# A graph and expert kernel: the second node stage joined with the making of its slot table, counts kept per tile

## What is computed

```
x = x + relu(segment_sum(norm * (layernorm(x) @ W.T + b)[row], col))
n = layernorm(x)
logits = einsum('td,hde->hte', n, hash_proj)      # 4 hashes, 64 experts
cand = argmax(logits, -1)                         # one candidate for a hash
sel = the candidates of the 2 best scores of the 4
pos = cumsum(one_hot(sel), axis=0) - 1            # place in its expert, tokens in order
keep = pos < C
y = gelu(n @ W1[e]) @ W2[e]                       # e = sel, kept ones only
x = x + mean over the 2 of y
```

## Time and profile before

| | us |
|---|---|
| median of 3 runs | 2936.8 (2929.69 to 2940.85) |
| the profiled execution, its time | 2943.63 |
| its span | 2941.9 |
| first node of the second node stage gathered (POOL) | 1726.38 |
| last entry of slot_tokens ends | 2266.93 |
| first gather of the expert stage | 2293.18 |

### The profile page before, as it was taken

How to read it: one execution, slowest core, us unless ns; L and a number is a source line. 1 busy time by engine, 2 the same in 40 slices (tenths; PEclk the granted TensorE clock), 3 DMA queues, 4 the chain that set the end, 5 groups by cost and what they waited for, 6 DMA issues and landing times. The chain is left out here.

```text
span 2941.9 us, 43922 instructions
## 1 busy us (share of the span) xinstructions
PE 2220.5 (75%) x11763; PEld 1308.8 (44%) x11789; DVE 1821.7 (62%) x5128; ACT 920.2 (31%) x2016; POOL 1789.1 (61%) x2143
## 2 busy tenths in 40 slices
PE   8999999857777728999978859999992677773000
PEld 3444444335555516666644436666661344442000
DVE  4776766524444459999921126777774477666666
ACT  1111111024445415777753315555552000000000
POOL 4555555566666348888536624777775555553776
PEclk9999999969898959999989979999996699897555
DMA  6655555468888646788669956666751799995999
GB/s 204 223 189 180 190 185 181 145 191 249 255 258 267 206 142 198 255 264 262 206 210 353 361 185 204 213 215 215 215 176 44 224 366 363 341 307 196 346 374 340
DMA packets 361398, 698.60 MB, mean 237 GB/s; under 512 B 51609, under 2 KB 85235, under 8 KB 361153
## 3 DMA queue, kind: packets, MB, share of 16 engines
q1 hardware_dynamic: 239672, 399.69, 40.0%
q0 software_dynamic: 76720, 217.93, 23.8%
q10 hardware_dynamic: 44761, 78.17, 7.5%
HBM read 426.08 MB, written 287.17 MB: 242 GB/s over the span
## 5 line engine op out<-in xcount | busy, mean ns | idle before, releaser
L2085 POOL DMA_INDIRECT xg<-n_rows,ids x219 | 218.3, 997 | 158.7 <-PE psum L154 81.1
L148 PE MATMUL psum<-wl,xT 128*128 128x512 f32 x632 | 288.8, 599 | 0.0
L148 PE MATMUL psum<-wg,yT 128*128 128x512 f32 x632 | 286.7, 597 | 0.0
L148 PE MATMUL psum<-wr,xT 128*128 128x512 f32 x632 | 284.1, 592 | 0.0
L2235 POOL DMA_INDIRECT q<-slot_outputs,qs x158 | 173.4, 1097 | 86.7 <-issue 47.9
L337 ACT ACTIVATE xb<-xa,xsc 128x512 f32<-128x512 f32 x79 | 64.2, 814 | 480.7 <-POOL xsc L397 480.6
L1637 POOL DMA_INDIRECT slot_tokens<-sl x158 | 169.1, 1070 | 66.0 <-issue 60.4
L154 PE MATMUL psum<-ident,xg 128*128 128x128 f32 x876 | 152.3, 308 | 71.6 <-issue 34.1
L384 POOL TENSOR_TENSOR ve<-mv,epst 128x1 f32<-128x1 f32 x79 | 51.0, 645 | 254.1 <-DVE mv L439 254.1
L2173 DVE COPY gT<-psum 128x512 f32<-128x512 f32 x219 | 142.0, 685 | 101.3 <-PE psum L154 54.2
L684 POOL DMA_INDIRECT gl<-xl_rows,idx x118 | 129.9, 1101 | 112.5 <-DVE vv L736 65.1
(11 more groups left out here) (320 smaller groups left out, 5497.2 us busy)
## 6 DMA issues: line engine op xcount, KB each, us to landing
slot_outputs<-yo ACTq DMA_DIRECT2D x54, 1024.0 KB
x_rows<-x SPq DMA_DIRECT2D x158, 256.0 KB
edge_sums<-eo SPq DMA_DIRECT2D x29, 1056.0 KB
edge_sums<-go SPq DMA_DIRECT2D x29, 1024.0 KB
xT<-in_xTt SPq DMA_DIRECT2D x79, 256.0 KB
xl_rows<-xl SPq DMA_DIRECT2D x79, 256.0 KB
xr_rows<-xr SPq DMA_DIRECT2D x79, 256.0 KB
residual_rows<-xb SPq DMA_DIRECT2D x79, 256.0 KB
```

Of the source, the lines that this page charges most:

```text
L148: last = nc.tensor.matmul(ps, lhs[:, k, :], rhs[:, k, :], start=(k == 0), stop=(k == DK - 1))
L2085: pool.indirect_dma_start(xg[:, t % 8, :], None, XN3, bass.IndirectOffsetOnAxis(ids[:, t:t + 1], 0), bounds_check=NP - 1, oob_is_err=False ...
```

## The change

- The slot table is made inside the second node stage: VectorE's 29 operations behind its last tile, reading the total of counts straight from TensorE's result (the copy cnt goes); POOL's two gathers of idr behind its last entry; TensorE's turning behind its last tile. One `end_phase` stands behind all.
- idr and xg are cleared at the beginning of the node stage, ahead of POOL's first gather of edge sums; the expert stage has no clearing.
- The sum of a group's rows (`counted`) goes. `count_up` keeps a running count for each tile, four small additions a group, cum having four places. So `before` has two products for a group, 256 columns wide, in the place of 14 of 64 columns.
- Order and lags: routing steps of a group stand in VectorE's steps 9 to 11 behind its tiles (10 to 13 today); `before` stands first in TensorE's step with lag 11 (last with lag 12 today); `enter` has lag 15 (18).

```diff
-        cnt = sb("cnt", [P, ME])
         cbase = sb("cbase", [P, ME])
         selk = sb("selk", [P, NT, 2])
         plk = sb("plk", [P, NT, 2])
+        trow = sb("trow", [1, 4 * P], I32)
+        ids = sb("ids", [P, 2 * P], I32)
+        xg = sb("xg", [P, 8, D])
...
-        osum = sb("osum", [P, ME], BF16, pe_)
-        cum = sb("cum", [P, 2, ME], BF16, pe_)
+        cum = sb("cum", [P, 2, 4, ME], BF16, pe_)
...
+                pool.memset(idr[:], 0).then_inc(e_lo, 1)
+                pool.memset(xg[:], 0.0).then_inc(e_lo, 1)
                 pool.wait_ge(e_i, 5)
-                pool.wait_ge(e_lo, 2)
+                pool.wait_ge(e_lo, 4)
...
-                tiles_in_turn(NT, ((0, later_rows), (6, minus_mean), (8, root), (18, enter)))
+                tiles_in_turn(NT, ((0, later_rows), (6, minus_mean), (8, root), (15, enter)))
+                pool.wait_ge(g_t, 1)
                 pool.wait_ge(e_id[0], 32 * NT)
+                for c in range(2):
+                    pool.indirect_dma_start(idr[:, c, :], None, IDX, bass.IndirectOffsetOnAxis(tid[:, c:c + 1], 0),
+                                            bounds_check=ME * SLOTS + LISTED - 1, oob_is_err=False)\
+                        .then_inc(g_ld, 16)
...
-                def counted(b):
-                    n = size(b)
+                def count_up(t):
+                    b = t // 4
                     dve.wait_ge(e_os, b + 1)
-                    with nc.allow_low_precision("counts up to 8"):
-                        nc.vector.tensor_reduce(osum[:], ohs[:, b % 2, 0:n, :].rearrange("p t e -> p e t"), AX.X, ALU.add)\
-                            .then_inc(e_ts, 1)
-
-                def count_up(b):
-                    dve.wait_ge(e_ts, b + 1)
-                    if b >= 1:
+                    if t >= 1:
+                        dve.wait_ge(e_cu, t)
+                    if t % 4 == 3 and b >= 1:
                         dve.wait_ge(e_pre, b)
-                    nc.vector.tensor_tensor(cum[:, (b + 1) % 2, :], cum[:, b % 2, :], osum[:], ALU.add).then_inc(e_cu, 1)
+                    nc.vector.tensor_tensor(cum[:, (t + 1) // 4 % 2, (t + 1) % 4, :], cum[:, b % 2, t % 4, :],
+                                            ohs[:, b % 2, t % 4, :], ALU.add).then_inc(e_cu, 1)
+
+                def count_on(j):
+
+                    def one(b):
+                        if 4 * b + j < NT:
+                            count_up(4 * b + j)
+                    return one
...
-                def g(f, late):
+                def g(f, lag):
 
                     def step(t):
                         if t % 4 == 3 or t == NT - 1:
                             f(t // 4)
-                    return (10 + late, step)
+                    return (lag, step)
 
                 tiles_in_turn(NT, (
-                    g(spotted, 3), (9, best_expert), g(compared, 0), g(counted, 2), (0, both), g(places, 3), (1, coefficient), g(tied, 0),
-                    g(one_hot, 1), (9, its_number), g(ahead, 0), g(count_up, 2), g(second, 3), (3, with_bias),
-                    g(choices, 1), g(ranks, 0), g(kept, 3), (5, residual), g(picked, 0), g(masked, 3), g(chosen, 0),
-                    g(weighed, 3)))
-                dve.wait_ge(e_w, NG4)
-                dve.wait_ge(e_tot, 1)
-                nc.vector.tensor_copy(cnt[:], bank[2][:, 0:ME]).then_inc(e_tot, 1)
-                dve.wait_ge(e_tot, 2)
...
+                    g(one_hot, 10), (9, best_expert), (0, both), g(choices, 10), (1, coefficient), (9, its_number),
+                    g(count_on(0), 10), (3, with_bias), g(compared, 9), g(count_on(1), 10), g(spotted, 11), g(tied, 9),
+                    g(count_on(2), 10), (5, residual), g(places, 11), g(ahead, 9), g(count_on(3), 10), g(second, 11),
+                    g(ranks, 9), g(kept, 11), g(picked, 9), g(masked, 11), g(chosen, 9), g(weighed, 11)))
+
...
+                dve.wait_ge(e_tot, 1)
                 then(nc.vector.tensor_scalar_mul(lim[:], iota[:, 0:SLOTS], float(P)))
-                then(nc.vector.tensor_scalar_min(cc[:], cnt[:], float(CAP)))
+                then(nc.vector.tensor_scalar_min(cc[:], bank[2][:, 0:ME], float(CAP)))
...
-            @block.gpsimd
-            def _(pool):
-                pool.memset(idr[:], 0).then_inc(g_rw2, 1)
-                pool.wait_ge(g_rw2, 1)
-                pool.wait_ge(g_t, 1)
-                for c in range(2):
-                    pool.indirect_dma_start(idr[:, c, :], None, IDX, bass.IndirectOffsetOnAxis(tid[:, c:c + 1], 0),
-                                            bounds_check=ME * SLOTS + LISTED - 1, oob_is_err=False)\
-                        .then_inc(g_ld, 16)
...
+                def before(b):
+                    n = size_of(b)
+                    ps = bank[2 + b % 2][:, 0:n * ME]
+                    pe.wait_ge(e_os, b + 1)
+                    pe.wait_ge(e_cu, 4 * b + n - 1)
+                    if b >= 2:
+                        pe.wait_ge(e_jk, b - 1)
+                    nc.tensor.matmul(ps, tri[:], ohs[:, b % 2, 0:n, :].rearrange("p t e -> p (t e)"), start=True, stop=False)
+                    nc.tensor.matmul(ps, onesb[:], cum[:, b % 2, 0:n, :].rearrange("p t e -> p (t e)"), start=False,
+                                     stop=True).then_inc(e_pre, 1)
...
+                tiles_in_turn(NT, ((11, groups), (1, turn_y), (7, logits), (6, turn), (2, gcn)))
+                pe.wait_ge(e_cu, NT)
+                pe.wait_ge(e_jk, NG4)
+                nc.tensor.matmul(bank[2][:, 0:ME], onesb[:], cum[:, NT // 4 % 2, NT % 4, :], start=True, stop=True)\
+                    .then_inc(e_tot, 1)
                 pe.wait_ge(g_t, 1)
+                pe.wait_ge(e_yT, NT)
...
+                pe.wait_ge(e_z, NT)
...
-                pool.memset(xg[:], 0.0).then_inc(p_0, 1)
-                pool.wait_ge(p_0, 1)
```

More of the change, by code:

```diff
@@ L1552, in gnn_ffn @@
         ehold = sb("ehold", [P, 4], F32, pe_)
+        lim = sb("lim", [P, SLOTS], F32, pe_)
+        cc = sb("cc", [P, ME], F32, pe_)
+        gt = sb("gt", [P, ME, SLOTS], F32, pe_)
+        ntl = sb("ntl", [P, ME], F32, pe_)
+        incl = sb("incl", [P, ME], F32, pe_)
+        le = sb("le", [P, 2, ME], F32, pe_)
+        lm = sb("lm", [P, 2, ME], F32, pe_)
+        tt = sb("tt", [P, 2, 3], F32, pe_)
+        tab = sb("tab", [P, 4], F32, pe_)
+        tid = sb("tid", [P, 2], I32, pe_)
+        idr = sb("idr", [P, 2, P], I32, pe_)
+        idf = sb("idf", [P, 2, P], F32, pe_)
+        g_c = sem("g_c")
+        g_ld, g_t, g_tr, g_rw, g_rw2 = (sem(n) for n in ("g_ld", "g_t", "g_tr", "g_rw", "g_rw2"))
         e_ld, e_lx, e_le, e_s3, e_sn, e_id = (
@@ L1866, in _ @@
+                nc.vector.tensor_copy(tid[:], tab[:, 0:2]).then_inc(g_t, 1)
+                dve.wait_ge(g_tr, 1)
+                nc.vector.tensor_copy(trow[:], bank[0][0:1, 0:4 * P]).then_inc(g_rw, 1)
+                dve.wait_ge(g_ld, 32)
+                nc.vector.tensor_copy(idf[:], idr[:]).then_inc(g_t, 1)
+                dve.wait_ge(g_tr, 2)
+                nc.vector.tensor_copy(ids[:], bank[1][:, 0:2 * P]).then_inc(g_rw, 1)
+                dve.wait_ge(g_rw, 2)
             @block.tensor
@@ L1895, in before @@
                     n = size_of(b)
+                    ps = bank[2 + b % 2][:, 0:n * ME]
                     pe.wait_ge(e_os, b + 1)
-                    if b >= 1:
-                        pe.wait_ge(e_cu, b)
+                    pe.wait_ge(e_cu, 4 * b + n - 1)
                     if b >= 2:
                         pe.wait_ge(e_jk, b - 1)
[L1901 to L1905, removed]
-                        last = nc.tensor.matmul(ps, onesb[:], cum[:, b % 2, :], start=False, stop=True)
-                    last.then_inc(e_pre, 1)
+                    nc.tensor.matmul(ps, tri[:], ohs[:, b % 2, 0:n, :].rearrange("p t e -> p (t e)"), start=True, stop=False)
+                    nc.tensor.matmul(ps, onesb[:], cum[:, b % 2, 0:n, :].rearrange("p t e -> p (t e)"), start=False,
+                                     stop=True).then_inc(e_pre, 1)
                 def size_of(b):
@@ L1915, in groups @@
                         before(t // 4)
-                tiles_in_turn(NT, ((1, turn_y), (7, logits), (6, turn), (2, gcn), (12, groups)))
-                pe.wait_ge(e_w, NG4)
-                pe.wait_ge(e_cu, NG4)
-                nc.tensor.matmul(bank[2][:, 0:ME], onesb[:], cum[:, NG4 % 2, :], start=True, stop=True)\
+                tiles_in_turn(NT, ((11, groups), (1, turn_y), (7, logits), (6, turn), (2, gcn)))
+                pe.wait_ge(e_cu, NT)
+                pe.wait_ge(e_jk, NG4)
+                nc.tensor.matmul(bank[2][:, 0:ME], onesb[:], cum[:, NT // 4 % 2, NT % 4, :], start=True, stop=True)\
                     .then_inc(e_tot, 1)
+                pe.wait_ge(g_t, 1)
+                pe.wait_ge(e_yT, NT)
+                for k in range(4):
+                    last = nc.tensor.matmul(bank[0][0:1, k * P:(k + 1) * P], tab[:, k:k + 1], ident[:],
```

(9 more changed lines are left out.)

91 lines of the change are left out of this document (26 added, 65 removed).

## The result

The changed kernel took 2905.5 us (median of 4 runs, 2897.4 to 2923.3), the kernel before 2933.3 beside it (4 runs): ratio 0.9908, 95% interval 0.9887 to 0.9928, so 21 to 33 us faster. Forecast were 2913 us (2900 to 2931) and faster. The profiled execution of the changed kernel is the longest of its four (span 2921.6). Against the profile before it is 20.3 us shorter: 29.7 us less from S, GpSimd's first instruction of the second node stage (1723.98 before, 1728.85 after), to the first gather of xg; against this 4.9 us more ahead of S, where the two programs do the same, 3.8 us more in the expert stage and 0.7 behind it.

A forecast was written before the change was run, and what follows sets the result against it. TensorE bounds the node stage's middle, GpSimd its run-out, DMA the expert stage. Terms +2.5 - 2.9 - 5.0 - 7.6 - 12.2 + 1.0 = -24.2 us give 2913 us, 8 in 10 within 2900 to 2931.

The forecast's parts named there:

- Beginning, +2.5: Node stage's start: idr and xg clearing delays the first gather; +2.5 us, bounds +1.1 to +3.8.
- Counting products, -2.9: TensorE: two wide products for 14 narrow save 0.17 us a group over 17 groups; -2.9 us, bounds -6.9 to +6.8.
- Run-out, first part, -5.0: GpSimd after TensorE's last tiles: last step with a square root ends about 5.0 us earlier, bounds -1.5 and -7.2.
- Six entries, -7.6: GpSimd's run-out: 16 entries instead of 22 behind the last root; -7.6 us, bounds -7.6 and -4.
- Joint, -12.2: Last entry's end to the expert stage's first gather: 26.2 us becomes 14.0; -12.2 us, bounds -13 and -9.
- Lost lead, +1.0: Expert stage: weight loads lose their 3.3 us start ahead of the first gather; +1.0 us.
- Rival 1: Middle of the node stage: GpSimd sets the pace and the good overlap may not return; 2926 us, chance 0.16.
- the rule on two SBUF inputs: VectorE instructions with two SBUF inputs block GpSimd's SBUF reads; three more of 0.17 us a group, priced under rival 1.
- Rivals 2 to 4: Run-out doesn't move, 2921 us (0.10); VectorE's group steps too long, 2952 us (0.06); table late, 2921 us (0.02).
- the pause: GpSimd's run-out: 2.51 us idle ahead of entries at 2215.41, put down to issue, unnamed; rival 2 has it stay.

The follow-up runs named there:

- narrow experiment: Changed kernel with 14 narrow counting products of 128x64 a group in place of two wide ones; ratio 0.9927 to the kernel before.
- Lag 18 with the new order: Changed kernel with the entry lag back at 18 instead of 15; ratio 0.9935 to the kernel before.
- join alone: Kernel before with only the table, idr gathers and transposes moved into the node stage and the idr and xg fills ahead; -0.35% against before.
- the kernel with the lead: Changed kernel without the join: table in its own stage, xg filled in the expert stage, as before; -0.55% against before.
- two experiments: Changed kernel with the xg fill back in the expert stage, 2898.5 us; changed kernel with 16 expert weight loads issued inside the node stage, 2901.7 us.
- VectorE's q fill: Changed kernel with the last stage's gather-tile fill cut into 12 pieces inside the expert stage; 2879.5 us against 2925.9 before, ratio 0.984.
- the large fill: Changed kernel with an added GpSimd fill of 128x1024 a tile in the second node stage; 2956.3 us.
- the two kernels with 79 fills more: Changed kernel with an added GpSimd fill a tile: 128x1024, 2956.3 us; or 128x64, 2789.5 us.
- the repeated kernel: Changed kernel run once more without an edit, in the last group of runs; 2786.3 us, ratio 0.9872.

## Why the prediction was right, step by step

From S to the first xg gather: forecast -25.2 (all terms but the lead), profiled -29.7. The direction and every place came as forecast; the largest term, the joint, was 2.6 us too small and lies outside the bounds that I gave it (-13 to -9).

- **Beginning, +2.5: mis-sized.** With the fill the first addition comes at S+9.63 to S+9.79 (seven profiles of the first three groups), without it at 8.74 to 9.02 (three): +0.8, by the third transpose some +0.4. My lower bound of +1.1 was the near end and should have been my value: its reasoning was right, a gather issued late is read 3.57 us after its issue (3.8 in my row), not 6.6. So most of the fill stands in time that the early gather spent waiting; that it waited for the other loads, as I wrote, no run shows.
- **Counting products, -2.9:** -3.3 up to the last transpose, with the beginning's cost in it; 3.9 in the narrow experiment. A group gave 0.22 us (period 24.59 to 24.37) and not 0.17, 17 groups 3.8. The way was right, the size a quarter too small. The cost of nothing for the earlier wait was right: TensorE has no idle time there.
- **Run-out, first part, -5.0:** the last root comes 34.0 us behind the last transpose instead of 38.3, -4.3. I had put it all to VectorE's wait. Lag 18 with the new order has 35.5, join alone with the old one 36.9: so 1.5 by the order and the products' place, 1.5 by the lag, which moves the pause out of the run-out, and 1.4 by neither, in join alone too; that last I can't name; the kernel before has one profile only.
- **Six entries, -7.6:** 28.6 us behind the last root became 21.2, -7.4.
- **Joint, -12.2:** -14.8. It stands below my bound of -13. The mis-sized piece is the 8.0 us of "landing, stage end and barrier": I left it whole, but what stands ahead of the idr gather now is the landing alone, 2.0, and stage end with barrier took 3.9 behind it, in the place where I had 8.0 + 0.6.
- **Lost lead, +1.0:** not shown. The first pair of profiles had the expert stage 3.8 us longer after, but inside the second group the kernel with the lead had the longest; leads given back (two experiments) changed no time.
- **Rival 1** (0.16) was nearer than its chance: the middle goes at TensorE's speed, but GpSimd has between 0.17 and 0.97 us a tile to spare, where its idle time seemed to say 1.5. My reason against it, that GpSimd "doesn't drift", held: with narrow products TensorE's 0.22 us a group came back at once. Of the rule on two SBUF inputs (the Trainium skill, page "SBUF — State Buffer", section on who interferes with whom) this kernel shows no price: GpSimd's busy time is 75.9 for 76.0 us in 100. Rivals 2 to 4 did not come: the pause stayed, as rival 2 said, but in covered time; VectorE kept pace (no idle time of TensorE); the table was ready 11 us ahead of the idr gather (2247.60 and 2258.82).

## What to carry to other kernels

At a barrier between stages, look for work ahead of the first transfer that needs nothing of the stage before or only its early results. There it stands in the path (the xg fill put the first gather 2.9 us later, VectorE's q fill 12.7); ahead of the node stage's first gather the xg fill cost 0.7 us, and in the middle of GpSimd's full list a fill was paid whole. An engine with a quarter of its time idle may have little room, if the idle time is "issue" between its own DMAs. Neither its idle time nor its waits for others say how much; a small dummy instruction does. A lag between producer and consumer decides how much stands behind the last tile; shortening it was worth 7.4 us for three tiles, and about 1.3 for one more, at which the consumer begins to wait.

## What the runs showed of the hardware that I had not expected

- GpSimd pauses at certain counts of its DMAs, not at a place of the program. Ahead of the 645th of 1055 there are 2.51 us with lag 18 and 2.61 to 2.65 with lag 15, in all thirteen profiles with these lags, though it stands at S+487 to S+491 with lag 18 and at S+468 to S+472 with lag 15 (530 with the large fill). This one is the first entry of tile 63 in all of them; the 553rd, with 2.80 to 2.85 us ahead of it in the same thirteen, is the first entry of tile 31 with lag 15 and of tile 30 with lag 18. It is no count of GpSimd's instructions either: the two kernels with 79 fills more pause at the same two DMAs. With lag 14 there were 1.62 us ahead of the 553rd and 1.55 ahead of the 644th. The cause is open.
- The same kernels ran 4% faster in the last group of runs (before 2818.2 us, else 2921.8 to 2933.3). The last three groups ran on three different chips, so chip and hour can't be told apart. Some 75 to 90 us of it lie ahead of S (1637.0 in the repeated kernel, 1711 to 1729 in the profiles of the other groups); these runs don't show why. The middle of the node stage, bound by TensorE, kept its 24.37 us to the hundredth; the expert stage, with the DMA engines busy 0.96 to 0.98 of it, was up to 35 us shorter. The repeated kernel's:

```profile
2176.00:2538.00 362.00, 265.37 (x3066) 170.36 (x3066) 272.95 (x438) 16.55 (x56) 218.92 (x219) 0.91 0.98 348
```

  348 GB/s for 320 in the changed kernel's first profile. Kernels are to be compared inside one group of runs, and a stage bound by transfers not by one profile each: inside one group it still ranged from 374 to 389 us.
